# Dividing the output side of a linear attention between two graph attentions: 13 node tiles beside the first, 12 beside the second, each tile over eight quads of edges

## The reference

```python
x = x + gnn(layernorm(x)) + mix(layernorm(x))
x = x + ffn(layernorm(x))

# gnn, two layers of attention over 53,125 edges, 8 heads of 64
scores = einsum('ehd,ehd->eh', q[tgt], k[srcidx])
p = exp(scores - segment_max(scores, tgt)[tgt])
w = p / (segment_sum(p, tgt)[tgt] + 1e-16)
agg = segment_sum(w[:, :, None] * v[srcidx], tgt)
attn = agg @ Wo.T + bo       # then batchnorm, feed-forward, batchnorm

# mix, linear attention over all nodes
q = softmax(proj(Wq, bq)); k = softmax(proj(Wk, bk)); v = proj(Wv, bv)
D_inv = 1.0 / (q * k_sum).sum(-1)
out = einsum('bhtd,bhde->bhte', q, context) * D_inv + q
return out @ Wp.T + bp
```

## Time and profile before

| | |
|---|---|
| median of 3 runs | 3036.39 us (3036.2 to 3044.52) |
| the profiled execution's own time | 3043.71 us |
| its span, first to last instruction | 3042.3 us |
| mean granted TensorE clock | 0.94 of 2.4 GHz |
| PE busy, 32,505 matmuls | 2609.1 us (86%) |
| DVE / ACT / POOL busy | 54% / 44% / 37% |
| DMA | 647.39 MB, mean 213 GB/s |

### The profile page before, as it was taken

How to read it: one execution, slowest core, us unless ns; L and a number is a source line. 1 busy time by engine, 2 the same in 40 slices (tenths; PEclk the granted TensorE clock), 3 DMA queues, 4 the chain that set the end, 5 groups by cost and what they waited for, 6 DMA issues and landing times.

```text
span 3042.3 us, 79016 instructions
## 1 busy us (share of the span) xinstructions
PE 2609.1 (86%) x32505; PEld 2127.2 (70%) x32505; DVE 1650.7 (54%) x3355; ACT 1325.4 (44%) x3694; POOL 1126.6 (37%) x1130
## 2 busy tenths in 40 slices
PE   5989997999999999678897788888888578589998
PEld 4867885877887878456686677777777465477777
DVE  5226776665665656646412455555555646666553
ACT  3323443555555555322232355555555322334432
POOL 0000002776776677100001377777777111122110
PEclk8999998999999999789998899999999889699998
DMA  5662003999999999540125499999999641122211
GB/s 197 230 255 99 31 29 131 349 346 330 342 347 335 340 339 342 188 131 16 49 97 215 165 355 345 353 352 352 355 351 351 210 118 55 38 94 91 70 60 60
DMA packets 233913, 647.39 MB, mean 213 GB/s; under 512 B 39072, under 2 KB 45856, under 8 KB 231491
## 3 DMA queue, kind: packets, MB, share of 16 engines
q0 software_dynamic: 137088, 466.78, 42.2%
q1 hardware_dynamic: 96451, 175.38, 16.8%
HBM read 551.60 MB, written 116.19 MB: 219 GB/s over the span
## 4 chain that ended last, share of the span: by engine, by line
PE 66%; DMA 14%; DVE 8%; issue 6%; POOL 2%; ACT 2%; SPq 1%; POOLq 0%; DVEq 0%; ACTq 0%
PE ps L1241 8%; PE ps L1284 5%; PE ps L1271 5%; PE ps L595 4%; PE ps L596 4%; PE ps L597 4%; DMA Y<-KVd,srcE 4%; PE ps L1248 2%; PE ps L997 2%; PE ps L999 2%; PE ps L998 2%; DMA Qd<-stage 2%; PE ps L1938 2%; PE ps L1940 2%; DMA WA<-KVd,srcE 2%
## 5 line engine op out<-in xcount | busy, mean ns | idle before, releaser
L1153 POOL DMA_INDIRECT Y<-KVd,srcE x360 | 342.2, 951 | 156.0 <-issue 64.9
L1435 ACT ACTIVATE stage<-ps,stage 128x128 f32<-128x128 f32 x832 | 294.1, 366 | 66.1 <-PE ps L1248 63.1
L1416 ACT ACTIVATE work<-ps 128x512 f32<-128x512 f32 x309 | 179.9, 596 | 282.1 <-PE ps L1241 281.6
L595 PE MATMUL ps<-Wh,xs 128*128 128x512 f32 x600 | 240.8, 401 | 56.1 <-DVE xs L535 56.1
L1416 ACT ACTIVATE G<-ps 128x512 f32<-128x512 f32 x315 | 183.0, 597 | 229.1 <-PE ps L1241 228.6
L1339 DVE COPY G<-ps 128x512 f32<-128x512 f32 x208 | 143.8, 691 | 252.3 <-PE ps L1248 246.3
L596 PE MATMUL ps<-Wl,xs 128*128 128x512 f32 x600 | 238.3, 397 | 0.0
L597 PE MATMUL ps<-Wh,xs 128*128 128x512 f32 x600 | 238.1, 397 | 0.0
L1153 POOL DMA_INDIRECT WA<-KVd,srcE x120 | 115.8, 965 | 323.1 <-PE ps L597 277.6
L1241 PE MATMUL ps<-ident,Y 128*128 128x128 f32 x1440 | 202.3, 279 | 32.3 <-DMA Y<-KVd,srcE 21.4
L1344 DVE TENSOR_REDUCE stage<-ps 128x4 f32<-128x512 f32 x208 | 143.8, 691 | 128.4 <-PE ps L1271 128.4
(11 more groups left out here) (405 smaller groups left out, 7123.8 us busy)
## 6 DMA issues: line engine op xcount, KB each, us to landing
KVd<-stage SPq DMA_DIRECT2D x96, 256.0 KB, 2.0
xTd<-xT SPq DMA_DIRECT2D x2, 6250.0 KB, 26.4
xT<-xTd SPq DMA_DIRECT2D x2, 6250.0 KB, 26.0
aggd<-work SPq DMA_DIRECT2D x6, 2048.0 KB, 7.4
Qd<-stage SPq DMA_DIRECT2D x48, 256.0 KB, 2.0
G<-aggd SPq DMA_DIRECT2D x48, 256.0 KB, 2.7
Y<-in_x SPq DMA_DIRECT2D x4, 1536.0 KB, 14.8
G<-mixq SPq DMA_DIRECT2D x24, 256.0 KB
```

The lines of the kernel that those rows point to most:

```text
L595: pe.matmul(PS[e % 4][0:r, :], xh, Wh[:, w, k, :], start=(k == 0), stop=False)
L1153: pool.indirect_dma_start(out=kvs[a], out_offset=None, in_=KVd[l][:, :], in_offset=bass.IndirectOffsetOnAxis(ap=srcE[:, n:n + 1], axis=0)) ...
L1416: act.activation(kT[n % len(kT)], banks(l)[place_of(l, "k", n) % len(banks(l))][:, :], ACT.Copy).then_inc(out_a, 1)
L1435: last = act.activation(pT[g % len(pT)][:, P * i:P * (i + 1)], SC[g % 2][:, P * i:P * (i + 1)], ACT.Exp, bias=smin[:, t:t + 1], scale=-1.0 ...
```

## The change

The output side's generators take the loop's number. `OUT_TILES` gives tiles 0 to 12 to the first loop and 13 to 24 to the second, and a tile takes 32 steps, so eight quads: 104 quads in the first loop, 96 in the second. All its step numbers are doubled or near it, so that on every engine the output side now stands at places 0 and 2 alone. The second loop gets three turn banks, since PS[0] and PS[1] are needed, its key buffers go from seven to six, its ring is laid out as the first loop's, and `early` goes from 9 to 4. The output weights are fetched and cut in two parts a second time, by a load that SP issues behind the one that puts x away. All semaphore counts behind this move along.

```diff
             else:
-                kvs = [mt[:, 512 + 1024 * i:1536 + 1024 * i] for i in range(2)] + [pair(rowsb, 2)] + spare + kvs + [
-                    pair(G, i) for i in (0, 2, 10)] + [pair(rowsb, 0)] + moved[0:3]
-                kT += [G[:, 12 + i, :] for i in range(4)]
+                kvs = [mt[:, 512:1536], pair(rowsb, 2)] + spare[0:2] + kvs + [pair(G, i) for i in (0, 2)] + moved
+                kT += [G[:, 12 + i, :] for i in range(3)]
...
-        TURN_BANKS, SC, AG = [[PS[4], PS[2], PS[3]], PS[0:5]], [PS[5], PS[6]], PS[7]
+        TURN_BANKS, SC, AG = [[PS[4], PS[2], PS[3]] for l in range(2)], [PS[5], PS[6]], PS[7]
...
-        OUT = 16
-        WpH, WpL, WP_CUT = WoH, WA2r, 24
+        OUT = 32
+        WpH, WpL, WP_CUT = WoH, WA2r, (24, 44)
+        OUT_TILES = [range(0, 13), range(13, NT)]
+
+        def out_steps(l):
+            return itertools.product(OUT_TILES[l], range(OUT))
...
+        def out_weights():
+            sp.dma_start(WA[:, 2], kpo(A["MpT"])).then_inc(g_in, 16)
...
-                if k == 3:
+                if k == 6:
                     pe.wait_ge(m_qe, t + 1)
...
-                if k == 7:
+                if k == 14:
                     pe.wait_ge(m_out, t + 1)
                     features(PS[1], t, ob, m_of)
-                if k >= 10 and k < 14:
-                    i = k - 10
+                if k in (20, 22, 24, 26):
+                    i = (k - 20) // 2
...
-            early = (4, 9)[l]
+            early = 4
...
                 is_normal(sp, 1, NCK - 1)
                 put_x(1)
+                sp.wait_ge(w2_mm, WO)
+                out_weights()
...
         attend_pool(1, begin1)
-        attend_pe(1, iter(()))
-        attend_dve(1, iter(()), begin1, work_free1)
-        attend_act(1, iter(()), begin1, work_free1)
+        attend_pe(1, sides[1])
+        attend_dve(1, sides[2], begin1, work_free1)
+        attend_act(1, sides[3], begin1, work_free1)
```

More of the change, by code:

```diff
@@ L741, in fetch_q, with out_sp @@
             sp.dma_start(qb[0:ROWS[t], :], mixq[P * t:P * t + ROWS[t], :]).then_inc(mq_in, 16)
-        def out_sp(views):
+        def out_weights():
+            sp.dma_start(WA[:, 2], kpo(A["MpT"])).then_inc(g_in, 16)
+        def out_sp(l, views):
             qT, oT, qb, ob, outb, Wp = views
[L745 to L752, removed]
+            if l == 0:
+                sp.wait_ge(qkv_mm, QKV_E)
+                out_weights()
+                sp.wait_ge(m_p, 3 * NT)
+                sp.wait_ge(m_r, 3 * NT)
+                sp.dma_start(rowsb[:, 1, :], A["mbp"].partition_broadcast(P)).then_inc(row_in, 16)
+                for i in range(2):
+                    sp.wait_ge(mq_st[i], 16 * uses(NT, 2, i))
+            else:
+                sp.wait_ge(qkv_mm, 2 * QKV_E)
+            fetch_q(OUT_TILES[l][0], qb)
             yield
-            for s in range(OUT * NT):
-                t, k = divmod(s, OUT)
-                if k == 8 and t + 1 < NT:
+            for t, k in out_steps(l):
+                if k == 16 and t + 1 in OUT_TILES[l]:
                     fetch_q(t + 1, qb)
-                if k == 15:
+                if k == 30:
                     sp.wait_ge(b_read, t + 1)
@@ L772, in out_pe @@
             yield
-            pe.wait_ge(g_in, 16)
+            pe.wait_ge(g_in, 16 * (l + 1))
             pe.wait_ge(m_bd, 1)
-            for s in range(OUT * NT):
-                t, k = divmod(s, OUT)
+            for t, k in out_steps(l):
                 r = ROWS[t]
@@ L812, in out_dve @@
             dve.wait_ge(row_in, 16 * 5)
-            for s in range(OUT * NT):
-                t, k = divmod(s, OUT)
+            for t, k in out_steps(l):
                 r = ROWS[t]
                 di = small[0:r, 24:32]
-                if k == 4:
+                if k == 8:
                     dve.wait_ge(m_c, t + 1)
@@ L832, in out_dve @@
                     dve.tensor_tensor(ob[0:r, :], ob[0:r, :], qb[0:r, :], ALU.add).then_inc(m_out, 1)
-                if t == 0 and k in (3, 5, 6, 7):
-                    i = (3, 5, 6, 7).index(k)
-                    dve.wait_ge(w_hi, WP_CUT + i + 1)
+                if t == OUT_TILES[l][0] and k in (6, 10, 12, 14):
+                    i = (6, 10, 12, 14).index(k)
+                    dve.wait_ge(w_hi, WP_CUT[l] + i + 1)
                     dve.tensor_tensor(WpL[:, i, :], Wp[:, i, :], WpH[:, i, :].bitcast(F32), ALU.subtract).then_inc(w_lo, 1)
-                if k == 9:
+                if k == 18:
                     dve.wait_ge(m_oe, 2 * t + 1)
@@ L846, in out_dve, with out_act @@
                 yield
-        def out_act(views):
+        def out_act(l, views):
             qT, oT, qb, ob, outb, Wp = views
             yield
-            for s in range(OUT * NT):
-                t, k = divmod(s, OUT)
+            for t, k in out_steps(l):
                 r = ROWS[t]
-                if k == 1:
+                if k == 2:
                     act.wait_ge(m_qf, t + 1)
@@ L863, in out_act, with out_done @@
                     act.activation(oT[0][:, :, 0:r], k4(PS[1][:, :])[:, :, 0:r], ACT.Copy).then_inc(m_oe, 1)
[L864 to L867, removed]
+                if t == OUT_TILES[l][0] and k in (4, 6, 8, 10):
+                    i = k // 2 - 2
+                    if i == 0:
+                        act.wait_ge(g_in, 16 * (l + 1))
+                    act.activation(WpH[:, i, :], Wp[:, i, :], ACT.Copy).then_inc(w_hi, 1)
                 yield
-        def out_done(e):
-            e.wait_ge(m_b, NT)
-            e.wait_ge(b_read, NT)
+        def out_done(e, l):
+            e.wait_ge(m_b, OUT_TILES[l][-1] + 1)
+            e.wait_ge(b_read, OUT_TILES[l][-1] + 1)
         ordb = ordE[:, :].rearrange("p (j x q) -> p j q x", x=2, q=4)
@@ L2109, in build @@
         ends_sp(0)
-        out_done(sp)
+        out_done(sp, 0)
         layer_weights(0)
@@ L2189, in work_free1 @@
             e.wait_ge(w2_mm, WO)
+        views = out_views(G)
+        sides = out_sp(1, views), out_pe(1, views), out_dve(1, views), out_act(1, views)
+        for side in sides:
+            next(side)
         attend_pool(1, begin1)
-        attend_pe(1, iter(()))
-        attend_dve(1, iter(()), begin1, work_free1)
-        attend_act(1, iter(()), begin1, work_free1)
+        attend_pe(1, sides[1])
+        attend_dve(1, sides[2], begin1, work_free1)
+        attend_act(1, sides[3], begin1, work_free1)
+        for side in sides:
+            for _ in side:
+                pass
         ends_sp(1)
+        out_done(sp, 1)
         layer_weights(1)
```

25 lines of the change are left out of this document (12 added, 13 removed).

## The result

The changed kernel takes 3061.39 us (median of 6 runs, 3053.64 to 3069.44) beside 3037.23 for the kernel before; the ratio is 1.0074, with a 95% interval of 1.0054 to 1.0093. The forecast was 3005, range 2985 to 3029.

A forecast was written before the change was run, and what follows sets the result against it. PE was taken to bound the first loop and POOL, issuing gathers, the second. First loop -50 us and second +19 (4 us between loops included) gave -31: 3013 profiled, 3005 for the median, range 2985 to 3029.

The forecast's parts named there:

- Output work at places 0 and 2 alone: Second loop: it puts DVE's 0.68 us subtraction one place later once in eight quads, priced at nothing.
- with DVE's waits left as they are: First loop: taking output work out of PE returns its full price, 5.1 us a tile, 61 us for twelve tiles.
- the sum's last step: Going from the profiled execution, 3013 us, to the median, taken as 7 us below it: 3005.
- The first loop: Twelve tiles fewer: end at 1204, 50 us earlier, bounds 1193 to 1217; PE alone gave 1193, POOL's pace 1196.
- The second loop: Twelve tiles more at POOL's 6.45 us a quad: end at 2405, 19 us later, bounds 2391 to 2416.
- 8 us for the coupling: Allowance in each loop for two near limits, PE's and POOL's, of which now one and now the other is late.
- Between the loops: Where x is put away: 1.57 MB less beside the query stores starts PE's query products 4 us earlier; bounds nothing to 6.
- Nine gathers of 0.52 MB run there: Beside the late query store: five go (2.6 MB), weights add 1.05 MB; its 26.89 us piece should be near 23.
- The five early gathers: Second loop: four early gathers in place of nine leave five more behind the first query tile, costing 6.2 us.
- The slower one: Rival, 0.07: new banks and coupling cost 64 us, 3069; sign: PE waits over 40 us for emptied banks, second loop.
- The rival by which the first loop doesn't give the time back: Rival, 0.09: output work may cover PE's waits for DVE, which then grow; 30 us less gain, 3035.
- The DMA rival: Rival, 0.14: DMA engines bound both loops at 348 GB/s, not POOL; loops end at 1217 and 2416, total 3029.

The follow-up runs named there:

- experiment 6: Kernel before, with only DVE's copy of a block's sums moved later, behind the key bank's emptying of the following even quad: 3015.85 us, ratio 0.991.
- experiment 3: Kernel before, with three turn banks and six key buffers in the second loop as well: 3040.77 us, ratio 1.0007.
- experiment 10: Kernel before, with the late copy of the block's sums and DVE's divide block one place later (step 5 for 4): 3012.83 us, ratio 0.9894.
- experiment 1: Changed kernel, with DVE's divide block moved from the start of a tile's third quad to the start of its fourth, an odd one: 3033.91 us, ratio 0.9983.
- experiment 2: Changed kernel, divide block behind DVE's key bank emptying in the odd fourth quad, subtraction and bias sum moved one place each: 3030.2 us, ratio 0.9965.
- experiment 9: Changed kernel, divide block in DVE's idle place of an odd quad, late copy of sums, output weights loaded at the second layer's products: 3015.38 us, ratio 0.9911.
- experiment 12: Kernel before, with four early gathers in the second loop in place of nine: 3047.3 us, ratio 1.0014.
- experiment 7: Kernel of experiment 1, with the second output weights load issued at the start of the second layer's products: 3034.1 us, ratio 0.9973 against the kernel before.
- experiment 5: Kernel of experiment 2, with DVE's copy of a block's sums moved behind the following even quad's key bank emptying: 3020.63 us, ratio 0.9923 against the kernel before.
- experiment 8: Changed kernel, divide block left in the even quad, with the copy of a block's sums moved later: 3021.62 us, ratio 0.9936.

## Why the prediction was wrong

**What bounds each loop** was read rightly: PE the first, POOL the second. Taking only waits of PE out of the first loop made it 22.8 us shorter (experiment 6), while experiment 3 and the second loops of experiments 6 and 10, where PE's work and waits matter least, all stay at 6.36 to 6.41 us a quad.

**The step that failed** is the one in the second loop's part, "Output work at places 0 and 2 alone", priced at nothing, with the first loop's "with DVE's waits left as they are". I followed the subtraction of 0.68 us that went one place later, and not the divide block, which kept its place 0 but went from an odd quad to an even one (step 4 of 16 is quad 1, step 8 of 32 is quad 2). There it stands behind a copy that is late itself and ahead of the bank that PE needs. Experiment 1 undoes that alone and makes the time 27 us less, more than the 24 by which the changed kernel is slower. The quads from 1222.90 to 1234.52 couldn't show it: they hold no output work on DVE.

**This step is half of the miss, not all of it.** The measured median is 56 us over the forecast, and with the block moved 25 to 29 us are left (3030.2 and 3033.91 for 3005). Experiment 2's profiled execution (3029.82 us) lies at its own median, so its stretches can be set beside the sum: the first loop ends at 1212.0 for 1204, the stretch between the loops takes 468.4 us for 460.4, from the query gather to the loop's end it is 693.2 for 690.5, and the rest is 1.5 shorter. These 17 us lead from 3013, the forecast for a profiled execution, to 3030. The other 8 are the sum's last step, which took off 7 us for the median (and 1 by rounding); in the later series the kernel before had medians of 3038.53 to 3042.19, and its profiled 3043.71 is only 2 to 5 us above them.

**The first loop** gave 17.9 us in the profile where 50 were forecast. With the block in an odd quad it ended at 1211.2, 43 earlier, and in experiment 2 42 earlier. So the sum's working for PE's part (5.1 us a tile) and POOL's limit came within 8 us once the wait was out. But part of the gain was never the tiles': with the copy late, the first loop is 22.8 us shorter with all 25 tiles in it, and dividing them gives only another 25.1 (experiments 6 and 9).

**The second loop** took 701.6 us from the first query gather for the forecast's 690.5 (2405 - 1714.5), and 687.5 and 693.2 with the block moved (experiments 1 and 2). From the gather on, the forecast was 23 us more than the 667.4 before (19 once the 4 us of the stretch between are taken off); 20 and 26 were measured. So this price, with POOL's 6.45 us and 8 us for the coupling, was about right once the wait is out.

**Between the loops** the sign was wrong: 3 us later, not 4 earlier. "Nine gathers of 0.52 MB run there" is true, but the query store stands in SP's queue, behind x and now behind the weights, and what POOL's queue holds doesn't delay it (experiment 12). The piece that was to fall from 26.89 us to 23 rose to 29.30. Experiment 7 shows the weights' place to be the 3 us.

**The five early gathers** were named as 6.2 us, but the sum holds 103 quads at 6.45 us, in which they are 5/4 x 6.45 = 8.1; experiment 12 shows 5 in the medians, 8.5 in the second loop of its profile.

**The rivals.** The slower one had 0.07 and ended on the right side, by another mechanism: not the three banks (experiment 3) but DVE's order. Its sign, over 40 us of waits for emptied banks in the second loop, was met: the two rows of PE at L1229 that name L1358 are 31.0 and 15.2 us there. The sign was a bad one, since the same rows are 33.7 and 15.1 us in the first loop, which had its three banks before as well, and experiment 1, with the same banks, takes 27 us off. The rival by which the first loop doesn't give the time back was met in size, 32 us less gain in the profile, but not in its mechanism: once the block is moved, the wait for the one-hot matrix is 41.8 us in 44 pieces (experiment 1, 580 us) for 38.7 in 42, and the loop ends 43 us earlier. The DMA rival falls in its form, a limit of 348 GB/s: the same bytes at 356 GB/s and a share of 0.97 give 3020 in experiment 5. Whether the DMA engines add to POOL's limit at these rates wasn't tried apart. The Trainium skill, DMA: Bandwidth & Descriptors, section Bandwidth, puts the HBM side of a core at about 358 GB/s, and says in the same section that a core gets about this when both cores of its HBM domain stream. This kernel uses one core, and its traces don't show 358 as a limit: the first loop of experiment 8 kept 357 GB/s over 580 us, and experiment 5 went over it for 100 us in its second loop (columns of the earlier trace rows), beside the 420 GB/s of the earlier trace rows.

```profile
2000.00:2100.00 100.00, 92.61 (x2013) 79.51 (x2009) 58.93 (x118) 62.04 (x196) 75.93 (x79) 1.00 0.98 366
```

**What stays open.** Experiment 1's profiled execution took 3021.14 us, the fastest of its 11 runs, whose median is 3033.91, so its stretches show more gain than its median. Experiments 1, 7 and 9 spread over 22 to 24 us from run to run, the other divided kernels over 10 to 16, and the kernel before over 17 among 29; which of the near limits makes that spread wasn't tried.

The waits of PE within the weighting of values (L1284, L1291 in the changed kernel), which grow whenever others go, are ended by no instruction of another engine. The traces show in part what they are. Beside the queues of the gathers and of SP the DMA view has one of a kind of its own, here for experiment 6 from 600 to 1200 (packets, MB, share of 16 engines):

```profile
q8 instruction: 93, 1.52, 1.0%
```

Its packets hold 16 KB and follow each other every 6.3 to 6.7 us on average in the first loops. I took their times from all fourteen traces. In the middles of both loops (600 to 1180 and 1800 to 2350) PE's weight loads at this line pause 364 times for over 0.3 us, and 362 of these pauses end 1.1 to 1.7 us after such a packet has ended, though stretches of that kind are only about a tenth of the time. 355 of them stand inside a set of matmuls, where the kernel waits for no semaphore. By this timing PE waits there for its own instructions to arrive. In 580 us of the first loop these pauses are 7.8 us in the kernel before, 9.6 in experiment 1, 12.5 in experiment 2 and 25.9 in experiment 5, so they take back a part of what the other waits give. Why the packets come too late, and whether the gathers' traffic beside them has a hand in it, wasn't tried.

## What to carry to other kernels

When side work is laid over a loop by step numbers, and the steps are stretched, check for each piece which of the loop's alternating iterations it now falls into and what the host engine owes others right behind it; doubling a step can turn odd into even. A copy that waits for another engine should stand behind the work that others wait for: moving one such copy gave 0.9% here, more than dividing 25 tiles. And before work is moved from a loop bound by one engine to one bound by another, ask what the first would then be bound by, and what the second has left: divided, both loops end at 6.5 to 6.6 us a quad (experiments 1, 2, 5 and 9), undivided with the copy late they take 6.76 and 6.41 (experiment 6), and the medians are the same.

## What the runs showed that I had not expected

A wait of 0.9 us and a block of 1.7 us, one behind the other on DVE, cost together far more than apart: with the copy out of the way the block's place in an even quad costs about 1 us in the medians (3021.62 and 3020.63 us), with the copy ahead of it 27 to 31 (3061.39 against 3033.91 and 3030.2). And a query store that shares SP's queue with 6.4 MB took 26.7 to 26.9 us in the chain with nine or with four gathers beside it in POOL's queue, but 29.3 us with one more MB ahead of it in its own.
